# A four-layer graph network: matrices moved with 128 partitions instead of 125, and GpSimd's byte copies started beside VectorE's share columns

## The reference

```python
x = layernorm(x + L0(x))   # 3 times: z = h + segment_sum(h[src], dst); z @ W1, batchnorm, relu, z @ W2
x = layernorm(x + L1(x))   # mean of x[dst] over src, two linears
x = layernorm(x + L2(x))   # mean of x[src] over dst, two linears, batchnorm
x = layernorm(x + L3(x))   # segment_max and segment_sum of weighted messages
```

## Time and profile before

| | us |
|---|---|
| median of three executions | 4169.85 |
| the profiled execution, its own time | 4173.97 |
| its span, first to last instruction | 4172.2 |
| around the span | 1.8 |
| VectorE busy in the span | 2545.4 |
| TensorE busy in the span | 3334.2 |
| GpSimd busy in the span | 2073.6 |

### The profile page before, as it was taken

How to read it: one execution, slowest core, us unless ns; L and a number is a source line. 1 busy time by engine, 2 the same in 40 slices (tenths; PEclk the granted TensorE clock), 3 DMA queues, 4 the chain that set the end, 5 groups by cost and what they waited for, 6 DMA issues and landing times.

```text
span 4172.2 us, 59104 instructions
## 1 busy us (share of the span) xinstructions
PE 3334.2 (80%) x21633; PEld 2948.1 (71%) x21633; DVE 2545.4 (61%) x6179; ACT 2081.1 (50%) x3413; POOL 2073.6 (50%) x1795
## 2 busy tenths in 40 slices
PE   1577767776755888689979999997478989899998
PEld 0466656665654888589969988996367777777776
DVE  7899999999973533478872225445334444444446
ACT  0566666666655444467775545555233333333321
POOL 2233333233237767577777810000677777777740
PEclk9888988898887999899989989998689999999999
DMA  4356565656563455733323322331447767767765
GB/s 136 102 166 183 174 183 181 186 163 184 172 176 79 174 192 192 245 129 124 123 69 141 129 108 92 129 128 57 128 146 238 250 235 262 256 241 255 246 230 178
DMA packets 297382, 707.35 MB, mean 170 GB/s; under 512 B 82284, under 2 KB 157459, under 8 KB 281860
## 3 DMA queue, kind: packets, MB, share of 16 engines
q1 hardware_dynamic: 196346, 546.33, 36.7%
q0 software_dynamic: 85408, 97.26, 9.7%
q10 hardware_dynamic: 15338, 59.95, 4.4%
HBM read 499.35 MB, written 252.62 MB: 180 GB/s over the span
## 4 chain that ended last, share of the span: by engine, by line
PE 28%; POOL 20%; DVE 17%; DMA 16%; issue 12%; ACT 6%; ACTq 1%; SPq 0%; DVEq 0%; POOLq 0%
POOL PAN L419 19%; DMA PAN<-counts 10%; PE PS L637 9%; PE PS L544 7%; DMA PAN<-turned 4%; DVE XP L1057 4%; PE PS L527 2%; PE PS L546 2%; DVE XP L1059 2%; PE PS L1664 2%; DVE CX L482 2%; ACT CX L472 2%; DVE DEG L958 1%; DVE SSB L484 1%; DVE CP L482 1%
## 5 line engine op out<-in xcount | busy, mean ns | idle before, releaser
L419 POOL DMA_INDIRECT PAN<-table,src_i x832 | 819.1, 984 | 784.7 <-DMA table<-DEG 506.7
L900 POOL DMA_INDIRECT shares<-dst_f,spare x832 | 857.2, 1030 | 334.9 <-issue 252.1
L544 PE MATMUL PS<-XR,BB 125*125 125x385 bf16 x2500 | 642.0, 350 | 215.7 <-issue 206.1
L863 POOL CAST PAN<-BB 125x6250 uint8<-125x6250 bf16 x50 | 272.1, 5442 | 761.4 <-ACT BB L753 761.4
L544 PEld LDWEIGHTS PS<-XR,BB 125*125 125x125 bf16 x2500 | 363.9, 146 | 299.4 <-issue 216.5
L546 PE MATMUL PS<-ident_h,BB 125*125 125x125 bf16 x2500 | 568.1, 227 | 0.0
L637 PE MATMUL PS<-CX,XH 125*128 125x376 f32 x2000 | 473.7, 319 | 96.6 <-DVE CX L482 33.9
L1059 DVE TENSOR_SCALAR XP<-iota_h,ST 128x250 bf16<-128x250 bf16 x1250 | 509.1, 408 | 0.0
L764 ACT ACTIVATE PAN<-PS 125x625 uint8<-125x625 bf16 x500 | 347.3, 695 | 296.5 <-PE PS L546 287.0
L753 ACT ACTIVATE BB<-PS 125x1000 bf16<-125x1000 f32 (+1 forms) x350 | 425.2, 1215 | 136.7 <-PE PS L527 133.3
L1750 ACT ACTIVATE BB<-PAN,ew 128x128 f32<-128x128 f32 x832 | 254.1, 388 | 455.8 <-DMA PAN<-table,src_i 455.8
(11 more groups left out here) (324 smaller groups left out, 6524.6 us busy)
## 6 DMA issues: line engine op xcount, KB each, us to landing
PAN<-counts SPq DMA_DIRECT2D x300, 381.5 KB
shares<-SSB SPq DMA_DIRECT2D x70, 1600.0 KB, 21.7
XP<-shares SPq DMA_DIRECT2D x50, 1600.0 KB
PAN<-shares SPq DMA_DIRECT2D x50, 1600.0 KB
BB<-start_penalty SPq DMA_DIRECT2D x104, 512.0 KB
shares<-blank ACTq DMA_DIRECT2D x15, 3200.0 KB, 14.3
counts<-PAN SPq DMA_DIRECT2D x50, 762.9 KB
turned<-PAN POOLq DMA_DIRECT2D x50, 762.9 KB, 18.6
```

The costliest lines, as they stand in the source:

```text
L419: nc.gpsimd.indirect_dma_start(out=gbuf[g % 2][:, k, :], out_offset=None, in_=source, in_offset=bass.IndirectOffsetOnAxis(ap=src_i[:, t:t ...
L544: nc.tensor.matmul(agg_wide, count_tile[t % 2][:, j, :], x_wide[0:TN, j, :], start=(j == 0), stop=False)
L900: nc.gpsimd.indirect_dma_start(out=shares_flat, out_offset=bass.IndirectOffsetOnAxis(ap=share_at[:, t:t + 1], axis=0), in_=share[:, t:t + ...
```

## The change

Three things are changed together.

- The stores of both matrices (`counts`, `turned`) and the loads of their panels move 128 partitions in place of 125 (`TN`). The last three rows carry no counts; nothing reads them after the load. So that they hold defined bytes, SyncE writes zeros over the rows 125 to 127 of `PAN` that no other data fills, in two small DMAs, and SyncE and GpSimd wait for them (`rows_blank`) ahead of the first store and the first byte copy.
- GpSimd's byte copy of a tile waits for a new semaphore, `bytes_turn`, that VectorE raises after `keep_rows` in each round.
- VectorE's two or three share parts of a round stand right behind that, in place of behind bundles 4 and 6 (and 1).

```diff
--- before.py
+++ after.py
@@ -116,7 +116,7 @@
                   for k in range(2)]
         count_tile = [w.rearrange("p (j d) -> p j d", d=TN) for w in
                       (BB[0:TN, 0:TW].bitcast(BF16), BB[0:TN, 3200:3200 + TW].bitcast(BF16))]
-        bytes_of = [PAN[0:TN, 1600 * u:1600 * (u + 1)].bitcast(U8)[:, 0:N].rearrange("p (s f) -> p s f", s=NBLK)
+        bytes_of = [PAN[:, 1600 * u:1600 * (u + 1)].bitcast(U8)[:, 0:N].rearrange("p (s f) -> p s f", s=NBLK)
                     for u in range(4)]
         stage, count_bytes = bytes_of[0:2], bytes_of[2:4]
         XP2F, CP = sb_with("XP2", ([128, 3200],), "CP")
@@ -270,6 +270,8 @@
         panel_summed = sem("panel_summed")
         turned_out = [sem(f"turned_out{u}") for u in range(2)]
         bytes_made = sem("bytes_made")
+        bytes_turn = sem("bytes_turn")
+        rows_blank = sem("rows_blank")
         tile_out = [sem(f"tile_out{u}") for u in range(2)]
         first_row = sem("first_row")
         x_in = sem("x_in")
@@ -497,10 +499,10 @@
                     sp.wait_ge(*cast_done(last))
                 c, s = divmod(u, NSUB)
                 if n == 3:
-                    sp.dma_start(panel[u % NPAN][0:TN, :], turned[c, 0:TN, s * TW:(s + 1) * TW]
+                    sp.dma_start(panel[u % NPAN], turned[c, :, s * TW:(s + 1) * TW]
                                  ).then_inc(panel_in[u % NPAN], 16)
                 else:
-                    sp.dma_start(panel[u % NPAN][0:TN, :], counts[c, s, 0:TN, :]).then_inc(panel_in[u % NPAN], 16)
+                    sp.dma_start(panel[u % NPAN], counts[c, s, :, :]).then_inc(panel_in[u % NPAN], 16)
 
         def hot_slot(t, m):
 
@@ -761,7 +763,7 @@
                 act.wait_ge(turns_full, n + 1)
                 if s == 0 and t > 1:
                     act.wait_ge(turned_out[t % 2], 16 * (t // 2))
-                nc.scalar.activation(stage[t % 2][:, s, :].rearrange("p (k n) -> p k n", k=SUBJ),
+                nc.scalar.activation(stage[t % 2][0:TN, s, :].rearrange("p (k n) -> p k n", k=SUBJ),
                                      turn_ps[n % 2][0:TN, :, 0:TN], ACT.Copy).then_inc(turns_kept, 1)
 
             def keep_columns(t):
@@ -808,6 +810,9 @@
             sp.dma_start(blank.rearrange("p (m f) -> p m f", m=8),
                          SSB[:, 0:800].unsqueeze(1).to_broadcast([128, 8, 800])).then_inc(blank_out, 16)
             zeros = SSB[:, 0:800].unsqueeze(1).to_broadcast([128, 4, 800])
+            sp.dma_start(PAN[TN:128, 0:3600].rearrange("p (m f) -> p m f", m=9),
+                         SSB[TN:128, 0:400].unsqueeze(1).to_broadcast([128 - TN, 9, 400])).then_inc(rows_blank, 16)
+            sp.dma_start(PAN[TN:128, 6096:6400], SSB[TN:128, 0:304]).then_inc(rows_blank, 16)
 
             def blank_part(c, r):
                 sp.dma_start(piece(shares, c)[:, r * 3200:(r + 1) * 3200].rearrange("p (m f) -> p m f", m=4),
@@ -816,13 +821,14 @@
             def store_tile(t):
                 sp.wait_ge(bytes_made, t + 1)
                 at = t % TPB * BLK
-                sp.dma_start(counts[t // TPB, :, 0:TN, at:at + BLK].rearrange("s p f -> p s f"),
+                sp.dma_start(counts[t // TPB, :, :, at:at + BLK].rearrange("s p f -> p s f"),
                              count_bytes[t % 2]).then_inc(tile_out[t % 2], 16)
 
             sp.wait_ge(pen_out, 32)
             for dst, src in ((half_dst, a["dst_half"]), (half_src, a["src_half"]), (half_w, a["ew_half"])):
                 sp.dma_start(dst, src).then_inc(halves_in, 16)
             blanks = 0
+            sp.wait_ge(rows_blank, 32)
             for t in range(NTILE):
                 store_tile(t)
                 while blanks < min(10 * ZBUILT, (t + 1) * 10 * ZBUILT // NTILE):
@@ -858,17 +864,19 @@
 
 
                 pool.wait_ge(hot_kept, NHOT * (t + 1))
+                pool.wait_ge(bytes_turn, t + 1)
                 if t > 1:
                     pool.wait_ge(tile_out[t % 2], 16 * (t // 2))
-                nc.gpsimd.tensor_copy(count_bytes[t % 2].rearrange("p s f -> p (s f)"),
+                nc.gpsimd.tensor_copy(count_bytes[t % 2][0:TN, :, :].rearrange("p s f -> p (s f)"),
                                       count_tile[t % 2].rearrange("p j d -> p (j d)")).then_inc(bytes_made, 1)
 
             def store_turned(t):
 
                 pool.wait_ge(turns_kept, NSUB * (t + 1))
-                pool.dma_start(turned[:, 0:TN, t * BLK:(t + 1) * BLK].rearrange("s p f -> p s f"), stage[t % 2]
+                pool.dma_start(turned[:, :, t * BLK:(t + 1) * BLK].rearrange("s p f -> p s f"), stage[t % 2]
                                ).then_inc(turned_out[t % 2], 16)
 
+            pool.wait_ge(rows_blank, 32)
             for t in range(NTILE + 1):
                 if t < NTILE:
                     make_bytes(t)
@@ -1120,9 +1128,12 @@
                             dve_half_weights(dve, h)
                     if m == 2 and 0 <= t - 2 < NTILE:
                         keep_rows(t - 2)
-                    if m in ((4, 6) if t % 4 else (1, 4, 6)) and 3 <= t < NTILE and shares_made[0] < T // GT:
-                        part(dve, shares_made[0])
-                        shares_made[0] += 1
+                    if m == 2 and 1 <= t <= NTILE:
+                        dve.sem_inc(bytes_turn, 1)
+                        for _ in range(2 if t % 4 else 3):
+                            if 3 <= t < NTILE and shares_made[0] < T // GT:
+                                part(dve, shares_made[0])
+                                shares_made[0] += 1
                     if t == NTILE and m == 3:
                         dve.wait_ge(hot_full, NHOT * NTILE)
                         dve.wait_ge(spare_ready, 1)
```

## The result

The kernel after takes 4127.58 us (median of four executions, 4122.74 to 4135.56). Beside it the kernel before took 4174.52 us (four, 4158.0 to 4180.2). The ratio is 0.9896, with a 95% interval of 0.9862 to 0.993: 1.0% faster, where the prediction said 2.2% (4078 us). The forecast range holds the time.

A forecast was written before the change was run, and what follows sets the result against it. It took VectorE to bound the build, nobody pass 1 (TensorE waits) and TensorE passes 2 to 4. Sum: 4174 - 0 - 62 - 14 - 16 = 4082, less 4 to the median, 4078 us; range 4000 to 4135.

The forecast's parts named there:

- A share part is held up by the copy: Build, VectorE: a part beside GpSimd's byte copy waits to the copy's end instead of taking its 2.17 us.
- The rival of 3907 us: Build: share parts are spared by the copy, rounds of 17.2 to 18.2 us, 171 us more gained; chance 0.09.
- Bundle 3 at K + 10.6, an idling of 4.8 us: Build round, counted from K, the end of keep_rows: VectorE has bundle 3 ready at 10.6 us; TensorE idles 4.8 us.
- The clock's price: Build: TensorE's lower clock after idling before bundle 3 costs 1.3 us a round, bounds nothing or 2.4; round 22.0, gain nothing.
- TensorE does not stay slow: Build: against a rival, chance 0.03, in which TensorE runs bundle 3 to the end at 1.2 GHz each round.
- The rival of 4258 us: Build: TensorE stays at 1.2 GHz from bundle 3 to the end, round 26 us, 180 us lost; chance 0.03.
- Sixteen engines for five: Panel transfers: 128 rows use 16 DMA engines where 125 use five; packets per panel go from 130 to 144.
- 76 expected: Passes 1 to 4: gains of 62 us in pass 1 and 14 us in passes 2 to 4.
- Pass 1: Panel loads on 16 engines gain 62 us, bounds 45 and 69; TensorE busy over 93%, a block 32 us.
- the 69 us: Pass 1: excess of its stretch over pass 2's pace, explained as ten blank slices at 7 us each.
- Passes 2 to 4: TensorE idles 66 us in their stretches; faster loads gain 14 us of it, bounds 4 and 25.
- The end of the build: ScalarE's waits for zero writes and a turned store shrink: 16 us gained, bounds 8 and 18; last landing some 17 us.

The follow-up runs named there:

- keep_busy: Kernel after plus 48 useless TensorE matmuls of 192 columns ahead of bundle 3 in each round from round 3 on: 4046.92 us, ratio 0.9698.
- stores_only: 128-partition kernel without the alignment, with all 400 panel loads back at 125 partitions and both stores kept at 128: 4115.95 us, ratio 0.9864.
- rows_only: Kernel after with share parts back at their old places and no byte-copy wait on VectorE, 128-partition stores and loads kept: 4027.75 us, ratio 0.9645.
- one_warm: Kernel after with one share part behind keep_rows, the other behind bundle 5, plus 24 useless matmuls ahead of bundle 3: ratio 0.9887, round 22.1 us.

## Why the prediction came out too fast

- **A share part is held up by the copy: right.** In each of the 45 rounds that have share parts, a `scalar_tensor_tensor` starts 0.4 us after the copy and takes 5.16 us; none is spared. The rival of 3907 us is out. (Its sum has a slip: rounds of 17.2 and 17.6 us with half of the clock's price make a mean of 18.0, not 18.2. Nothing hangs on it.)
- **Bundle 3 at K + 10.6, an idling of 4.8 us: right**, 10.9 and 5.1 us (over the build K + 11.4, where 11.15 was forecast with the rounds of three parts). A lump of work went to the place where VectorE was held up anyway, and the forecast that this wins nothing on its own held.
- **The clock's price, 1.3 us a round: this step failed, by its size.** It was taken from one row with 2.24 us of idling (1.6 us lost), and set a little below. Behind 5.1 us of idling, bundle 3 to the end of the sums took 11.3 us in the round shown, and 10.0 in the next, where the forecast has 8.6 for a warm TensorE: 2.7 and 1.4 us. The mean of 42 rounds is 10.7, so the price is 2.1 us. With bundle 3 at K + 11.4 and 0.9 us for `keep_rows` this is the measured round: 11.4 + 10.7 + 0.9 = 23.0. Of the 1.0 us that it is above the forecast 22.0, 0.8 is the clock and 0.25 is bundle 3, a little later than worked out. That it is the clock is shown by keep_busy: there it stays up, bundle 3 to the end of the sums takes 8.4 us, and the round is 20.95. The bounds of the term, nothing or 2.4 us (a loss of 50 us), did hold the truth near their upper end: +48.3 us stand in the build where the sum has 0. That is nearly the whole miss (49.5 us from 4078 to 4127.6).

  Rows with a longer idling stood in the trace of the kernel before, in TensorE's timeline:

```profile
1130.75 0.55 PE L544 MATMUL PS<-XR,BB 125*125 125x385 bf16 x1 [9.20 <-issue]
...
1132.91 1.04 PE L527 MATMUL PS<-XP 128*125 128x250 bf16 x4
...
1135.86 0.33 PE L544 MATMUL PS<-XR,BB 125*125 125x385 bf16 x1
```

  TensorE is slow for 5.1 us here. At half speed that is an estimated 2.5 us lost, which is near the price of 2.1 us and nearly twice the 1.3 taken. In the kernel before it cost little: there VectorE is busy 927 of 985 us, and TensorE's sums lie done for some 9 to 12 us in every second round.
- **TensorE does not stay slow: right.** The rival of 4258 us needed 1.2 GHz to the end of the sums. In the round shown the third bundle behind the wait (1167.79) is at 0.59 us again. But it stays slow longer than in the row that spoke against the rival: there the next bundle was back at 0.59 us, here it still takes 1.04.
- **Sixteen engines for five: right.** In pass 4, with no other traffic, the queue of SyncE moved this (packets, MB, share) in 290 us:

```profile
q1 hardware_dynamic: 12194, 33.86, 39.5%
```

  33.86 MB are 84.7 panels of 400,000 bytes, so 144 packets each, as forecast. The passes gained 53.5 + 21.2 = 74.7 us for 76 expected; stores_only puts 79 us on the loads.
- **Pass 1 is not as clean as forecast.** TensorE is busy 85% of 400 us, 0.92 clock; that stretch reaches beyond the pass, and in 1344 to 1690 us, within it, it is 307 of 346 us (89%), where over 93% was forecast. A block takes 33 to 37 us, not 32. The chain that ended last has one such entry in most blocks:

```profile
1475.44 13.31 DMA PAN<-counts
...
1508.16 13.90 DMA PAN<-counts
...
1541.46 15.14 DMA PAN<-counts
```

  Each is about as long as a blank slice takes to land (14.5 us). So the slices seem to hold up the panels still, and this is the likely reason why 8.5 of the 62 us did not come; no run varied the slices. The forecast itself was not clean here: it has a slice hold the engines for 14.3 us and then counts 7 us for each, which is the 69 us of the rows divided by ten and not a figure worked out by itself. Passes 2 to 4 gave 21 for 14, inside their bounds.
- **The end of the build: 12.4 us for 16.** The last zero write lands 21.9 us behind the end of the last copy (1284.6 - 1262.7), where the sum had 17. With no queue before it it still took 20.8 us from its issue, where 14.9 is the median of such writes; it was issued right behind the store of the last tile and one more zero write:

```profile
1257.29 5.41 POOL PAN L870
...
1263.80 20.79 DMA shares<-SSB
```

- **The issue of the turned store: not in the prediction at all.** Its price of 1.98 us was taken as given at 128 rows. It fell to 0.95 us and is worth 45 us in rows_only, where VectorE is bound and held up beside it. In the kernel after it is worth nothing, since a share part is not held up by an issue, as the prediction had said of that part. The sum for the kernel after did not miss it; a forecast for the 128 partitions alone would have. With it the two halves of the change are: 128 partitions alone -147 us (4174.5 to 4027.8), the alignment on top of them +100 us (4027.8 to 4127.6), 93 of them at the last byte copy. With 125 partitions it costs less, 43 us at the last copy and 1.07% of the time; the likely reason is that there it also hides an issue of 2 us. The rounds say the same, 22.0 to 22.85 us with 125 and 21.0 to 23.0 with 128.

## What to carry to other kernels

Before you fill one engine's stall with a lump of work, ask who waits for what comes behind the lump: here VectorE's filled 6 us became 5 us of TensorE idling, and the slower matmuls behind it cost 2.1 us a round, as much as lies between the rounds of rows_only (21.0) and of the kernel after (23.0). When the clock's price is taken from a row, take a row with as long an idling as the new one, or else let the bound carry the forecast. Do one half of such a change at a time: rows_only is some 2.5% faster than both together.

## What the runs showed of the hardware that was not expected

- GpSimd issued the direct store from 128 partitions in 958 ns and the one from 125 in 2007 ns (50 of each, in kernels that differ in little else); VectorE's `tensor_scalar` beside it took 0.73 against 1.63 us. The median from issue to landing fell from 18.6 us before to 12.0 after, and the packets of that queue from 85408 to 66208.
- Useless matmuls made a kernel 81 us faster (4046.92 against 4127.58), at a granted clock of 0.99 in place of 0.87 in the build. In one_warm, 24 of them made it slower.
- After 5.08 us of idling TensorE ran at half speed for 6.0 us (1160.38 to 1166.36), and in the next round, after as much, for 3.4 us (1183.41 to 1186.80). After 2.79 us its first bundle was as slow in one round (1.09 us, 1082.47) and not in another (0.64 us, 1019.76), where the slow stretch began 0.7 us later. After 1.12 us, with the useless matmuls ahead, it took 0.64 us.
